# Attention blocks on one core: the rows of the maximum are sent by GpSimd instead of SyncE, and the replicas are issued in another order

## What is computed

```python
# first two blocks, T = 1024, ch = 16
h = group_norm(x) * gamma + beta
q, k, v = split(W_qkv @ h + b)                       # per head: 16 x 1024 each
w = softmax(einsum('bct,bcs->bts', q*scale, k*scale))
out = x + W_proj @ einsum('bts,bcs->bct', w, v) + b_proj
```

## Time and profile before

| | us |
|---|---|
| median of 3 runs | 2487.98 |
| lowest, highest | 2482.21, 2491.14 |
| the profiled execution | 2498.52 |
| its span, first to last instruction | 2496.8 |
| of it the images of the first two blocks, about | 0 to 1914 |
| TensorE, VectorE, ScalarE, GpSimd busy | 2173.1, 1743.4, 1657.4, 458.5 |

### The profile page before, as it was taken

The page is one execution under the profiler, slowest core; times in us unless marked ns, Lnnn a source line. Parts: engine busy times, 40 slices in busy tenths (PEclk is TensorE's granted clock), DMA queues, the critical chain, the costliest instruction groups (busy, mean ns, idle before and its releaser), DMA issues. The chain is left out here.

```text
span 2496.8 us, 32884 instructions
## 1 busy us (share of the span) xinstructions
PE 2173.1 (87%) x11778; PEld 1069.3 (43%) x11778; DVE 1743.4 (70%) x2115; ACT 1657.4 (66%) x3009; POOL 458.5 (18%) x682
## 2 busy tenths in 40 slices
PE   1888879897888988797978889888988999999999
PEld 0333323333333333233333333333332788888887
DVE  1776768685776867675857668676761777777776
ACT  0366657574666666575757667665765888888887
POOL 4102011110202020111101020201000333333331
PEclk7699999897989998888979899989995999999999
DMA  5144251505052341515050523415100111111111
GB/s 76 15 57 60 43 74 42 87 20 83 25 78 49 54 70 33 77 39 85 18 87 24 79 43 60 65 37 74 43 24 27 53 62 61 53 49 51 61 49 45
DMA packets 56101, 133.00 MB, mean 53 GB/s; under 512 B 13600, under 2 KB 24992, under 8 KB 55968
## 3 DMA queue, kind: packets, MB, share of 16 engines
q1 hardware_dynamic: 55968, 131.27, 28.7%
HBM read 53.12 MB, written 17.83 MB: 28 GB/s over the span
## 5 line engine op out<-in xcount | busy, mean ns | idle before, releaser
L485 DVE TENSOR_REDUCE h_half_nmax<-h_s_ps 128x2 f32<-128x1024 f32 x1024 | 1207.2, 1220 | 451.0 <-PE h_s_ps L666 446.7
L599 ACT ACTIVATE h_probs<-h_st_ps 128x512 f32<-128x512 f32 x2048 | 1069.1, 602 | 543.5 <-PE h_st_ps L773 527.7
L773 PE MATMUL h_st_ps<-h_qrep,h_krep 51*128 51x512 f32 x2048 | 690.3, 504 | 209.4 <-DMA h_qrep<-h_mrow 179.6
L773 PEld LDWEIGHTS h_st_ps<-h_qrep,h_krep 51*128 51x128 f32 x2048 | 294.4, 197 | 783.1 <-ACT h_probs L599 434.3
L656 PE MATMUL h_pv<-h_probs,h_vT 128*32 128x512 f32 x4096 | 591.8, 652 | 0.0
L666 PE MATMUL h_s_ps<-h_krep,h_qrep 48*128 48x512 f32 x2048 | 397.3, 448 | 74.3 <-SPq L237 30.5
L666 PEld LDWEIGHTS h_s_ps<-h_krep,h_qrep 48*128 48x128 f32 x2048 | 211.5, 203 | 185.9 <-DVE h_half_nmax L485 87.2
L1295 PE MATMUL o_s<-o_k,o_q 128*128 128x512 f32 x768 | 223.9, 428 | 8.1 <-DVE o_q L1116 5.7
L378 POOL TENSOR_SCALAR h_nparts<-h_nmax 128x16 bf16<-128x16 f32 x64 | 16.3, 255 | 1131.0 <-DVE h_nmax L492 1131.0
L1295 PE MATMUL o_pv<-o_pT,o_vT 128*128 128x512 f32 x768 | 207.3, 406 | 0.8 <-ACTq L1222 0.8
L1110 DVE TENSOR_TENSOR o_pT<-o_t,o_pT 128x512 fp32r<-128x512 f32 x256 | 164.5, 684 | 42.4 <-ACT o_pT L1247 38.9
(11 more groups left out here) (106 smaller groups left out, 1247.6 us busy)
## 6 DMA issues: line engine op xcount, KB each, us to landing
h_krep<-h_kp SPq DMA_DIRECT2D x96, 256.0 KB, 9.2
h_qrep<-h_qp SPq DMA_DIRECT2D x96, 256.0 KB, 18.1
x_res<-out_dram SPq DMA_DIRECT2D x24, 512.0 KB, 3.7
num<-av SPq DMA_DIRECT2D x128, 64.0 KB
rrep<-rden_dram SPq DMA_DIRECT2D x16, 512.0 KB
out_dram<-o_y SPq DMA_DIRECT2D x16, 512.0 KB
out_dram<-h_y SPq DMA_DIRECT2D x15, 512.0 KB, 2.7
o_x_in<-out_dram SPq DMA_DIRECT2D x15, 512.0 KB, 3.6
```

The lines of the kernel that those rows point to most:

```text
L485: reduce = nc.vector.tensor_reduce(half_nmax[:, c, th, :, pair % MP], s_ps[slot][:, :, :], AX.X, ALU.max, negate=True)
L599: nc.scalar.activation(probs[g % 2][:, j, :], st_ps[n % COLUMN_BANKS][:, :], ACT.Exp, scale=1.0 / CH ** 0.5).then_inc(columns_done, 1)
L773: nc.tensor.matmul(st_ps[n % COLUMN_BANKS][:, :], krep[par][part, quad * 2 + m, st * P:(st + 1) * P], qrep[par][part, quad * 2 + m, th * H ...
```

## The change

The rows of the maximum are issued by GpSimd, each time right behind the `split_max` that they come from, and it waits there for ScalarE's copy. The layout of `qrep` becomes [partition, half, pair, 512] and that of `nparts` follows, so that the rows of one `r` are one DMA of 24 rows to 3 partitions: two DMAs for each half instead of four. The queries are therefore replicated by twelve DMAs of half the size. SyncE's `replicate` is taken apart: keys are issued right behind the read of `rrep`, without a wait for it; the wait of `spread` (`spread_done`) follows, then the queries and the wait for all replicas. VectorE's `invert` moves from k=6 to k=5. The counter `mrow_dma` is never lowered: TensorE waits for growing values.

```diff
-        qrep = [sb(f"qrep{i}", [P, HEADS // 2, T], F32R) for i in range(2)]
+        qrep = [sb(f"qrep{i}", [P, 2, HEADS // 2, HALF], F32R) for i in range(2)]
@@ SyncE
+            def replicate_keys(par, n):
+                sp.wait_ge(parts_ready, n)
+                for term, part in enumerate((0, 0, 1)):
+                    for r in range(2):
+                        to, of = r * ROWS + term * CH, slice(r * ROWS, (r + 1) * ROWS)
+                        sp.dma_start(krep[par][to:to + CH, :, :].bitcast(F32),
+                                     parts["k"][of, part, :].bitcast(F32)).then_inc(rep_dma, 16)
+            def replicate_queries(par, n):
+                sp.wait_ge(parts_ready, n)
+                for term, part in enumerate((0, 1, 0)):
+                    for r in range(2):
+                        to, of = r * ROWS + term * CH, slice(r * ROWS, (r + 1) * ROWS)
+                        for th in range(2):
+                            sp.dma_start(qrep[par][to:to + CH, th, :, :].bitcast(F32),
+                                         parts["q"][of, part, th * HALF:(th + 1) * HALF].bitcast(F32)).then_inc(rep_dma, 16)
+            def replicated():
+                sp.wait_ge(rep_dma, 16 * 6 * TERMS)
@@ SyncE, body
+                    if of_image_before:
                         sp.wait_ge(av_ready, 2 * u + 1)
                         last_output(image(i - 1))
                         sp.wait_ge(rden_ready, u + 1)
                         spread()
-                    max_rows(4 * u + 1, u, 0, 1)
-                    if not (last and u == 1):
-                        replicate(1 - u, u)
-                    max_rows(4 * u + 2, u, 1, 0)
+                    if more:
+                        replicate_keys(1 - u, 2 * u + 1)
+                    if of_image_before:
+                        spread_done()
+                    if more:
+                        replicate_queries(1 - u, 2 * u + 2)
+                        replicated()
...
-                    max_rows(4 * u + 3, u, 1, 1)
-                    if not (last and u == 1):
-                        max_rows(4 * u + 4, 1 - u, 0, 0)
@@ GpSimd
+            def max_rows(n, par, quad, th):
+                pool.wait_ge(mrow_ready, n)
+                for r in range(2):
+                    pool.dma_start(qrep[par][r * ROWS + KS:r * ROWS + KM, th, quad * 2:(quad + 1) * 2, :].bitcast(F32),
+                                   mrow[th][r * MAX_PARTS * MP:(r + 1) * MAX_PARTS * MP, :].bitcast(F32)).then_inc(mrow_dma, 16)
@@ GpSimd, body
                     split_max(4 * u + 1, 1)
+                    max_rows(4 * u + 1, u, 0, 1)
                     if not (last and u == 1):
                         split(2 * u + 2, "q")
                     if first and u == 0:
                         pool.sem_inc(o_in, 1)
                     else:
                         normalise(u + 1)
                     split_max(4 * u + 2, 0)
+                    max_rows(4 * u + 2, u, 1, 0)
                     split_max(4 * u + 3, 1)
+                    max_rows(4 * u + 3, u, 1, 1)
                     if not (last and u == 1):
                         split_max(4 * u + 4, 0)
+                        max_rows(4 * u + 4, 1 - u, 0, 0)
                         coefficients(u)
@@ VectorE
-                        if s % 2 == 0 and k == 6:
+                        if s % 2 == 0 and k == 5:
@@ TensorE
-                            pe.wait_ge(mrow_dma, 64 * (2 * s + k // TILES + 1))
+                            pe.wait_ge(mrow_dma, 32 * (8 * pair + 2 * s + k // TILES + 1))
```

More of the change, by code:

```diff
@@ L172, in many_heads @@
         idle = sb("idle", [P, 2])
-        nparts = [sb(f"nparts{i}", [P, 2, 2, MAX_PARTS, MP // 2], BF16) for i in range(2)]
+        nparts = [sb(f"nparts{i}", [P, 2, MAX_PARTS, MP], BF16) for i in range(2)]
         mrow = [sb(f"mrow{i}", [MAX_PARTS * MH, P], F32R) for i in range(2)]
@@ L237, in replicate @@
+            def replicated():
+                sp.wait_ge(rep_dma, 16 * 6 * TERMS)
+                sp.sem_inc(rep_dma, -16 * 6 * TERMS)
                 sp.sem_inc(rep_ready, 1)
                 sp.sem_inc(parts_free, 1)
[L240 to L247, removed]
@@ L257, in _ @@
             sp.wait_ge(ones, 1)
-            replicate(0, 0)
+            replicate_keys(0, 1)
+            replicate_queries(0, 2)
+            replicated()
             sp.sem_inc(parts_ready, -2)
@@ L295, in body @@
                     i = 2 * pair + u
[L297 to L300, removed]
+                    of_image_before = not (first and u == 0)
+                    more = not (last and u == 1)
+                    if of_image_before:
                         sp.wait_ge(av_ready, 2 * u + 1)
@@ L304, in body @@
                         spread()
[L305 to L308 removed]
+                    else:
+                        sp.sem_inc(av_ready, 1)
+                        sp.sem_inc(rden_ready, 1)
+                    if more:
[4 more added lines that the diff above has]
+                        replicate_queries(1 - u, 2 * u + 2)
+                        replicated()
                     sp.wait_ge(y_ready, 2 * (u + 1))
@@ L374, in split_max @@
                 pool.wait_ge(nmax_ready, n)
-                new = nmax[:, th * MH:(th + 1) * MH].rearrange("p (m t) -> p m t", t=MP // 2)
-                left = nrest[:, :].rearrange("p (m t) -> p m t", t=MP // 2)
-                to = nparts[th][:, :, :, :, :].rearrange("p r m a t -> p (r m) a t")
+                new = nmax[:, th * MH:(th + 1) * MH].rearrange("p (r m) -> p r m", r=2)
+                left = nrest[:, :].rearrange("p (r m) -> p r m", r=2)
+                to = nparts[th]
                 own.done(nc.gpsimd.tensor_scalar(to[:, :, 0, :], new, 1.0, None, ALU.mult))
@@ L392, in _ @@
             pool.sem_inc(nmax_ready, -1)
+            max_rows(1, 0, 0, 0)
+            pool.sem_inc(mrow_ready, -1)
             coefficients(1)
@@ L665, in row_scores @@
                     rows = slice(r * ROWS, r * ROWS + KS)
-                    product = nc.tensor.matmul(s_ps[slot][:, r, :], qrep[par][rows, m, th * HALF + tile * P:th * HALF + (tile + 1) * P],
+                    product = nc.tensor.matmul(s_ps[slot][:, r, :], qrep[par][rows, th, m, tile * P:(tile + 1) * P],
                                                krep[par][rows, m, c * HALF:(c + 1) * HALF], start=True, stop=True)
@@ L703, in _, with body @@
             pe.sem_inc(nparts_ready, -1)
-            def body(first=False, last=False):
+            def body(pair, first=False, last=False):
                 columns, rows = places(last)
@@ L773, in column_scores @@
                             nc.tensor.matmul(st_ps[n % COLUMN_BANKS][:, :], krep[par][part, quad * 2 + m, st * P:(st + 1) * P],
-                                             qrep[par][part, quad * 2 + m, th * HALF:(th + 1) * HALF],
+                                             qrep[par][part, th, quad * 2 + m, :],
                                              start=True, stop=True).then_inc(columns_ready, 1)
```

10 lines of the change are left out of this document (4 added, 6 removed).

## The result

| | before | after |
|---|---|---|
| median, us | 2486.59 (4 runs, 2482.21 to 2491.14) | 2450.16 (4 runs, 2447.45 to 2452.49) |
| span of the profiled execution, us | 2496.8 | 2449.5 |

The ratio is 0.9853 with a 95% interval of 0.9831 to 0.9875: 31 to 42 us faster. The forecast was 2260 us, 2230 to 2350. The sign was right, the size was not: 36 of the 228 us came, 1.5% of the time.

The account below looks back on a forecast made before the run. TensorE (87% busy) was taken as the bound, waiting 179.6 us for rows of the maximum. Ceiling 250 less 22 for what is left of stop A saves 228: 2270.5 profiled, 2260 us as median, range 2230 to 2350.

Parts of the forecast that it names:

- The ceiling of 250 us: Most that freeing TensorE of both stops and their clock loss could save, taken from two estimates, 252 and 260 us.
- the undisturbed image: First image without its stop B and the slowed groups behind it: 105.1 - 6.3 - 1.8 = 97.0 us.
- What a stop costs in clock: After a stop TensorE works at the lower clock level, losing 4.9 us per image, some 72 in 15.
- GpSimd's issue at 1 us for each DMA: Cost of GpSimd issuing each row DMA, taken as 1 us between bounds of 0.77 and 3.5 us.
- Rows at k=5: GpSimd sends stop A's rows; they meet the keys' transfer, land at 560.8 to 569.5, leaving 1.5 us of stop (0 to 7.6).
- Stop A: TensorE's wait for rows of the maximum before group 8 of the even step, 7.83 us; forecast to fall to 1.5 us.
- the 0.91 share of the windows: DMA engines' busy share while replicas move, at 102 GB/s; used to price one 4 KB packet at 0.58 us.
- Rival 1: Rows alternate piece by piece with the keys; stop A stays 4 to 7.6 us, time 2333 to 2387; chance 0.22.
- Rival 2: GpSimd's rows served only when SyncE's packets have run out; stop A 24 us, B none, time about 2660; chance 0.05.
- Stop B: TensorE's wait for rows before group 0 of the odd step, 4.79 us; forecast to go to 0, at most 2 us.
- The queries' twelve DMAs: Twelve 2 KB-row DMAs instead of six: 3.9 us more issue time, covered by the keys' transfer; 0 to 4 us once.
- The earlier reciprocal: `invert` moves from k=6 to k=5 into VectorE's idle 1.46 us, so spread and keys are issued earlier.

Follow-up runs that it names:

- the 2245 us version: Changed kernel with keys issued only after the rows for k=8 have landed and eight of twelve query DMAs after the odd step's rows; 2244.7 us, 0.9025 of the kernel before.
- the runs with ScalarE and with two queues: Changed kernel with the rows for k=8 issued by ScalarE, 2542.1 us; or one of their two DMAs from GpSimd and one from ScalarE, 2476.3 us.

## Why the prediction was wrong

- What bounds the kernel, and the two stops: right. Taking both away gives 2245.
- The ceiling of 250 us: near. 2488 - 250 = 2238, measured 2244.7 with 3.1 us of waiting left; the undisturbed image was put at 97.0 us and is 97.7.
- What a stop costs in clock (72 us in 15 images; 13.7 x 0.36 x 15 is 74): right in size. In the 2245 us version 177 us of waiting are gone and 240 of time, which leaves 63; TensorE's busy time is 79 us less there (2094.1 for 2173.1) for the same instructions.
- GpSimd's issue at 1 us for each DMA: two take 1.23 us, so 0.6 each, less than SyncE's 0.77. Landing undisturbed was put 3.3 us behind the first issue; the pair lands after 2.7. Both as taken or better.
- The step that failed is the price of sharing in "Rows at k=5". It was put at one packet of 0.6 us, up to 9.3 us at most, and taken at 1.5 us of stop. The measured delay behind GpSimd's issue is 16.9 us instead of 3.3 without sharing: the rows wait for most of what SyncE has issued ahead of them (1.6 MB in most images), not for one packet. Stop A came out at 11.7 us, beyond the 7.6 of the range. And the first image, in which the prediction had no stop A, got one of 4.5 us by the same sharing. That makes (11.7 - 1.5) x 15 = 153 us of waiting and, with 6.1 x 0.36 = 2.2 us of lost clock in each image, 33 more: 186 of the missing 190. Where I went wrong is that the 0.91 share of the windows told me the engines were full, and I priced what a new transfer would add to one packet, when what counts above all is what is queued ahead of it.
- Rival 1 named the sharing, but as turns piece by piece, and was too small (stop A 4 to 7.6 us, 2333 to 2387; measured 11.7 and 2450). Rival 2, rows served only when SyncE's packets have run out, is nearer in kind: that is how the rows land in the first image. But it priced keys and queries as one block (stop A 24 us), and in the other images the rows get through before the keys have ended. The Trainium skill (DMA: Bandwidth & Descriptors, Issuing engines are not separate DMA queues) has the rule that bears on it, that all engines' DMAs share the same DMA engines. The prediction set it aside as one of bandwidth; the runs with ScalarE and with two queues agree with it.
- Stop B: 0 as forecast, but for another reason, so this hit is luck. The prediction had B's rows go out about 6 us ahead of the end of the replicas and gave them 4 us for sharing. That is the same mis-sized step: wherever stop A is gone and the replicas still run, B's rows take 10 to 14 us and B is back with 2.5 to 7.5 us. In the changed kernel it is 0 because stop A puts its rows off.
- The queries' twelve DMAs, GpSimd's order, the layout: at nothing, as put. GpSimd's `normalise` starts at 561.49, while TensorE still waits for group 8, `coefficients` are not late, and TensorE's first wait for the replicas is 30.4 us as before.
- The earlier reciprocal was counted as hidden, which it is, and only as what makes the keys meet the rows. Left where it was, it leaves 2361: 89 us of the missing gain.

## What to carry to other kernels

A small DMA on which the critical engine waits has to be issued ahead of large ones, in time, not on another queue: a queue of its own saved the wait in program order here but not the wait behind what was already queued (16.9 us), and it gave up the place ahead of the keys that SyncE's own order gives (5.7 to 6.7 us). Before a large transfer is moved earlier, list the small ones that go out in the time it takes, and hold it back for them if it has slack; here two waits on the transfer's issuer were worth 205 us. As a first estimate, price sharing by what is queued ahead of the transfer at its issue, divided by the rate, not by one packet.

## What the runs showed of the hardware that I had not expected

- Two DMAs of 12 KB have landed 2.7 us after their first issue when alone, and 16.9 us after it when issued amid 2.1 MB on another queue. To TensorE's start it is 23.0 us from ScalarE's queue and 19.8 from two queues (one run each).
- The delay grows with the amount queued (4.4, 11.2, 15.9, 16.9 us for 0.5, 1.0, 1.6 and 2.1 MB), and halving the size of SyncE's packets for the keys took off only 2.3 of the 16.9 us (one run).
- GpSimd issues a DMA of 24 rows in 0.6 us, faster than SyncE one of 12 or of 24 (0.77 us; two of 24 in 1.58).
- With no stop longer than 1.6 us, TensorE kept the upper level of its clock, 2.4 GHz, through fourteen images (granted clock 1.00 over 1368 us).
